# A two-layer sequence model on one NeuronCore: the four step inputs of a scan tile move from GpSimd to VectorE

## The reference

```python
u = silu(conv(xc) + conv_b)                     # 512 channels
dt = softplus(dt_low @ dt_proj_w.T + dt_proj_b) # the step size
A = -exp(A_log)                                 # 512 channels x 16 states
def step(hstate, t):
    dA = exp(dt_t[..., None] * A)
    hstate = dA * hstate + (dt_t * u_t)[..., None] * B_t[:, None, :]
    y_t = einsum('bdn,bn->bd', hstate, C_t)
    return (hstate, y_t)
y = (ys + u * D) * silu(z)
```

## Time and profile before

| | |
|---|---|
| median of 3 runs | 3255.33 us (3255.09 to 3268.93) |
| profiled execution | 3253.97 us, span of its instructions 3252.2 us |
| busy over the span | TensorE 2604.3 (80%), VectorE 2312.8 (71%), GpSimd 2041.2 (63%), ScalarE 2010.5 (62%) |
| TensorE's mean granted clock | 0.906 |
| scans L1327 | 1024 instructions, 1241.8 us busy, 1264 ns each |
| weighings L1508 on GpSimd | 256, 1157.5 us, 4535 ns each |
| dbu L1500 on GpSimd | 128, 580.3 us, 4533 ns each |
| dbu L1336 on VectorE | 128, 289.7 us, 2263 ns each |
| first and last step input L1514 | 1306.7 us and 3173.7 us, 64 of them |

### The profile page before, as it was taken

One profiled execution on the slowest core, in us unless ns is written; L12 is line 12 of the kernel. 1 busy time (PEld: TensorE's weight loads), 2 busy tenths in 40 slices (PEclk: granted clock), 3 DMA queues, 4 the chain that ended last, 5 costly groups with the idle time before them and its releaser, 6 DMA issues.

```text
span 3252.2 us, 44230 instructions
## 1 busy us (share of the span) xinstructions
PE 2604.3 (80%) x13178; PEld 1491.6 (46%) x13178; DVE 2312.8 (71%) x2761; ACT 2010.5 (62%) x3265; POOL 2041.2 (63%) x641
## 2 busy tenths in 40 slices
PE   7773257776777725799999999999989999999987
PEld 3331113222333222465655655665655655565555
DVE  5553444444555261889889889889889889889995
ACT  2221124444444402788779779778879778888874
POOL 3333110000000000899999989999989999999996
PEclk9886668888888867799999999999999999999999
DMA  5554165555545111232132133133132132133020
GB/s 152 146 148 113 32 161 162 162 162 162 161 143 154 29 47 59 111 111 94 44 112 105 34 111 105 34 112 105 34 113 103 34 120 98 43 113 111 34 98 7
DMA packets 135223, 323.49 MB, mean 99 GB/s; under 512 B 13361, under 2 KB 90417, under 8 KB 118594
## 3 DMA queue, kind: packets, MB, share of 16 engines
q1 hardware_dynamic: 115730, 250.03, 25.7%
q0 software_dynamic: 18560, 70.20, 5.7%
q10 hardware_dynamic: 688, 0.23, 0.1%
HBM read 277.25 MB, written 43.13 MB: 99 GB/s over the span
## 4 chain that ended last, share of the span: by engine, by line
PE 24%; issue 12%; POOL 11%; ACT 6%; DVE 6%; ACTq 1%; DVEq 1%; DMA 0%; POOLq 0%; SPq 0%
PE l_p_w L1853 10%; POOL l_st L1508 7%; PE l_p_y L1845 5%; PE l_p_w L1899 4%; DVE l_st L1327 4%; POOL l_st L1500 3%; PE l_p_w L1918 3%; ACT l_p_a L1577 2%; POOL l_dtu L1514 1%; DVE l_st L1336 1%; ACT L1652 1%; PE l_p_w L1906 1%; ACT L1586 1%; DVE l_stats L1343 1%; ACTq L52 1%
## 5 line engine op out<-in xcount | busy, mean ns | idle before, releaser
L1327 DVE TENSOR_TENSOR_SCAN l_st<-l_p_a,l_hl,l_st 128x512 f32<-128x512 f32 x1024 | 1241.8, 1264 | 116.2 <-ACT l_p_a L1577 96.3
L1508 POOL TENSOR_TENSOR l_st<-l_st,l_cs 128x2048 f32<-128x2048 f32 x256 | 1157.5, 4535 | 16.4 <-ACT l_hl L1582 16.2
L1577 ACT ACTIVATE l_p_a<-l_dt,l_a_neg 128x512 f32<-128x512 f32 x1024 | 666.2, 681 | 57.4 <-DVE l_st L1327 52.7
L1500 POOL TENSOR_TENSOR l_st<-l_bs,l_dtu 128x2048 f32<-128x2048 f32 x128 | 580.3, 4533 | 50.0 <-PE l_p_y L1845 46.1
L1845 PEld LDWEIGHTS l_p_y<-l_ident,l_st 128*128 128x128 f32 x4096 | 471.0, 145 | 157.6 <-issue 78.3
L1845 PE MATMUL l_p_y<-l_ident,l_st 128*128 128x128 f32 x4096 | 507.2, 280 | 44.2 <-POOL l_st L1508 44.2
L739 DVE TENSOR_REDUCE a_mpart<-a_p_m 128x1 f32<-128x512 f32 x512 | 320.0, 683 | 303.5 <-PE a_p_m L842 301.1
L798 ACT ACTIVATE a_pr<-a_p_s 128x512 f32<-128x512 f32 x512 | 283.6, 595 | 222.5 <-PE a_p_s L876 221.3
L717 POOL DMA_DIRECT2D a_w<-in_w_dram x32 | 22.4, 707 | 535.3 <-PE a_p_m L894 534.2
L876 PE MATMUL a_p_s<-a_qst,a_kst 99*128 99x256 bf16 x1024 | 220.4, 308 | 144.3 <-DMA a_qst<-a_nT 92.6
L1336 DVE TENSOR_TENSOR l_st<-l_bs,l_p_u 128x2048 f32<-128x2048 f32 x128 | 289.7, 2263 | 9.6 <-issue 7.6
(11 more groups left out here) (220 smaller groups left out, 3242.0 us busy)
## 6 DMA issues: line engine op xcount, KB each, us to landing
a_w<-in_w_dram POOLq DMA_DIRECT2D x64, 1024.0 KB, 17.3
l_bs<-s_bc SPq DMA_DIRECT2D x64, 1024.0 KB, 4.7
l_cs<-s_bc SPq DMA_DIRECT2D x64, 1024.0 KB, 5.0
l_xt<-s_x SPq DMA_DIRECT2D x32, 512.0 KB, 4.4
s_kp<-t_kp SPq DMA_DIRECT2D x96, 128.0 KB
a_kst<-s_kp SPq DMA_DIRECT2D x16, 768.0 KB, 7.9
s_vp<-t_vo SPq DMA_DIRECT2D x16, 544.0 KB
a_vg<-s_vp SPq DMA_DIRECT2D x16, 544.0 KB, 13.4
```

Source lines behind the costliest of these rows:

```text
L1327: eng.tensor_tensor_scan(st[k % NG][:, n, :], p_a[:, n, :], st[k % NG][:, n, :], hl[:, k, n:n + 1], ALU.mult, ALU.add).then_inc(scan_ok, 1)
L1500: eng.tensor_tensor(st[n][:, :, :], bs[:, 4 * n:4 * n + 4, :], dtu[(k // NG) % 2][:, :].unsqueeze(1).broadcast_to([P, NG, TT]), ALU.mult). ...
L1508: eng.tensor_tensor(st[n][:, :, :], st[n][:, :, :], cs[:, 4 * n:4 * n + 4, :], ALU.mult).then_inc(cm_ok, 1)
L1577: eng.activation(p_a[:, n, :], dt[c % 2][:, :], ACT.Exp, scale=a_neg[:, c, m:m + 1]).then_inc(dA_ok, 1)
```

## The change

`step_input` goes from GpSimd's list to VectorE's, with the same three waits and the same signal. In VectorE's `period` each of the four calls stands right behind the `step_size` of its block; for block 0 that is the period of the tile's front, where it used to stand near the start of the next one. GpSimd's other work keeps its order. The instruction's line is L1382 in the new kernel, and GpSimd's lines move on by some lines: dbu from L1500 to L1510, the weighing from L1508 to L1518, the residual from L1519 to L1523.

```diff
+                def step_input(t, pt, c):
+                    taken(eng, "dt", t, c)
+                    wait(eng, dtp_ok, t * CB + c - 1)
+                    wait(eng, dbu_g, t * 8 + 2 * c - 2)
+                    eng.tensor_tensor(dtu[c % 2][:, :], dt[c % 2][:, :], u[pt][:, c, :], ALU.mult).then_inc(dtu_ok, 1)
...
                         step_size(s, 1)
+                        step_input(s, o, 1)
...
                         step_size(s, 2)
+                        step_input(s, o, 2)
...
                         step_size(s, 3)
+                        step_input(s, o, 3)
...
                         step_size(q, 0)
+                        step_input(q, p, 0)
...
-                def step_input(t, pt, c):
...
-                        step_input(s, o, 0)
...
-                        step_input(s, o, 1)
...
-                        step_input(s, o, 2)
...
-                        step_input(s, o, 3)
```

More of the change, by code:

```diff
@@ L1528, in period @@
                         dbu(f, 15)
-                    if scan:
-                        step_input(s, o, 0)
                     if front:
```

## The result

The changed kernel takes 3409.53 us in the median of 4 runs (3409.23 to 3414.36); the kernel before, run beside it, 3259.47 us (3255.09 to 3268.93). The ratio is 1.046, with a 95% interval of 1.0432 to 1.0488: slower by 150 us, where 71 were forecast. The direction and the cause held, the size did not, and 3409.5 lies above the range of 3250 to 3390. The profiled execution has a span of 3407.5 us, 155.3 more than before.

The account below looks back on a forecast made before the run. Four engines pace each other. Passing 6.8 us a tile less 0.9 gained gives 83 us over 14 tiles, or 62 with GpSimd standing elsewhere; the middle, 72, on 3254.0 gives 3326 us, range 3250 to 3390.

Parts of the forecast that it names:

- What bounds the kernel: Second layer's tiles, 121.5 us each: four engines pace each other; a microsecond taken from one is worth little.
- the sum had 13: GpSimd's relief: TensorE's long wait for it goes, 0.9 us a tile over 14 tiles, about 13 us.
- The price that decides: Whether the SBUF-only multiply runs beside GpSimd: 0.83 us if so, else the rest of GpSimd's instruction; the upper was taken.
- Rival (a): Nothing blocks: the multiply stays near 0.7 us beside GpSimd, 19 us gained, 3235 us; chance 0.15.
- Rival (b): The multiply blocks but meets GpSimd idle or late more often, and gaps hold: about 3262 us; chance 0.10.
- (c): GpSimd's next instruction goes ahead of the blocked multiply, a two-instruction wait at two places a tile: 3452 us; chance 0.05.
- The sum: Multiply's lateness at four places a tile, less gaps and relief: 5.9 or 4.4 us a tile; middle 72 us.
- what is queued behind: Behind the inputs: scans that ScalarE's exponentials wait for; gaps take up part, 6.8 us a tile pass, before 0.9 gained.
- the step from 83 to 72 us: GpSimd will stand elsewhere after the change: 4.4 us a tile, 62 us; the middle with 83 is 72.
- Input 1 I take to cost nothing: Stretch behind input 1 is paced by TensorE's up, turn and down products, so its mean 2.9 us costs nothing.
- Behind input 0 stand 1.75 us: 2.18 pass: VectorE's 1.75 us gap behind input 0 absorbs part of its 3.93 us lateness; 2.18 us a tile pass.
- terms of 2.14 and 2.48: Microseconds a tile passed on behind inputs 2 and 3, after gaps take up part of 4.06 and 3.28 us lateness.

Follow-up runs that it names:

- e7: Kernel before, with GpSimd's step inputs from the second tile on cut to 64 of 512 elements: 3249.68 us against 3256.36, ratio 0.9979.
- e4: Kernel before, with step input 1 alone moved to VectorE: 3298.21 us, ratio 1.0113, 40.3 us over before.
- e11: Kernel before, input 0 alone moved, as a PSUM multiply behind a 2632-element reduction (product with u left out except first tile): 3305.18 us, ratio 1.0122.
- e12: Changed kernel, with TensorE repeating gate products in its two long waits behind inputs 0 and 3: 3388.84 us, ratio 1.0412.
- e1: Changed kernel, with the multiply's second input read from PSUM tile p_u in place of u, except the first: 3258.11 us against 3258.61 before, ratio 0.9995.
- e8: Changed kernel, with each multiply but the first issued twice, the earlier into a spare tile: 3695.15 us, ratio 1.135.
- e9: Kernel before, plus a stretch ahead of the second layer with 250 GpSimd multiplies beside 128 VectorE multiplies at all phases: 4441.4 us with the stretch.

## Why the prediction was right in kind and wrong in size

**What bounds the kernel** was right: four engines pace each other, and relief on GpSimd is worth little (7 us by e7, where the sum had 13).

**The price that decides** was right, and so were its prices but for input 1: 4.06, 3.28, 3.93 and 2.9 us forecast for inputs 2, 3, 0 and 1; 4.20, 3.45, 3.85 and 1.84 measured. The multiply ends 0.55 us behind GpSimd's end, where 0.44 was worked out from the first stage's L225. The rule of the Trainium skill, "SBUF — State Buffer", section "Who interferes with whom", holds here with its number: with two SBUF inputs 61 of 64 multiplies meet a GpSimd instruction and end behind it, with one of them in PSUM none of 63 waits. Who comes next is another matter: the 13 multiplies above waited for GpSimd instructions that started after them. Rival (a) is thereby dead, by the operand's place and not by the instruction's kind. Rival (b) fell with the lengths; (c) did not occur in the changed kernel, though its mechanism exists (13 of 57 meetings with one input moved alone).

**The sum** is where it failed, in the passage "what is queued behind". It passed on 5.1 us a tile (72 over 14) of about 14 us of lateness; the trace has 9.9 of 13.3. Part of this is the step from 83 to 72 us: it let GpSimd stand elsewhere after the change, with a lateness of 2.85 us at inputs 3 and 0, but 3.45 and 3.85 were measured. The larger part is what was said to be taken up behind the inputs.

- "Input 1 I take to cost nothing": alone it costs 40 us (e4), with a lateness of 3.39 us, most of it from multiplies that GpSimd passed over. The prediction has the stretch behind it paced by TensorE's products, but the turn product there waits for a ScalarE copy that stands behind the held exponentials.
- "Behind input 0 stand 1.75 us: 2.18 pass": alone, without a meeting, 45 us in place of 30.5 (e11). The gap is in VectorE's list, 14 us further on; the delay leaves VectorE before it, through ScalarE's exponentials and gate row, and comes back to it. ScalarE's queue was named by the prediction ("scans, for which ScalarE's exponentials wait") and not followed to the row behind them.
- Behind inputs 2 and 3 the steps come closer: 32 us measured for 30, and 52.5 for 34.7, of which the one multiply of 14.20 us in the traced run explains some 10. In the steady tiles 1.6 and 2.2 us pass for terms of 2.14 and 2.48, so the near agreement of input 2's total is in part luck, and no run shows that the gaps named there took up the rest.
- Missing altogether was TensorE's clock. Waits of 4.19 and 2.97 us are followed by matmuls at 0.50, 1.5 and 1.8 us longer a tile; TensorE's busy time over twelve tiles rose from 1350.8 to 1391.2 us. Filling the waits gave 17 to 21 us back (e12). The forecast counted TensorE's waits as time and no more.

The four places alone add up to more than the change costs (45 + 40 + 32 + 52 = 169 against 150): in the changed kernel input 1 meets less of a GpSimd instruction (1.84 us late, against 3.39 alone), and no multiply is passed over. The terms by place, the clock and the 17 us that only the meeting brings overlap, so they are no sum to the microsecond. No experiment gave a usable version faster than the kernel before: reading PSUM (e1, without the product with u) only comes back to it, and e7, 7 us faster, leaves out most of the product.

## What to carry to other kernels

Before a VectorE instruction is given two SBUF inputs beside a busy GpSimd, price it at the rest of GpSimd's instruction plus its own length, at every place where it stands, and reckon that GpSimd's next instruction may go first (13 of 57 meetings with one input moved alone). In this kernel one operand in PSUM freed it. A gap absorbs a delay only if it lies on the way from the delayed instruction to the engine that paces the end: follow the delay through the other engines' lists, in order, since a gap on the delayed engine's own line may be the far end of the same loop. Where a new wait makes TensorE stand, as the 2.97 and 4.19 us did here, look at the granted clock behind it too.

## What the runs showed of the hardware

A GpSimd instruction that starts while a blocked multiply still has to run is itself held: 4.97 us in place of 4.53, in 47 of the 256 weighings of the changed kernel. The two engines took turns, one instruction each, in the changed kernel, in e8 and in e9. With one input moved alone 13 of 57 multiplies let GpSimd instructions go first that started after them: nine let one by, three two and one three. What decides is open. And useless matmuls in a wait made a kernel 17 to 21 us faster, since the ones behind them then ran at the full clock.
